# A gated cross-attention layer on one core: query blocks eight ahead of the units instead of nine, and the first output chunk split beside query blocks

## The reference, cut to what matters

```python
def _L0_xattn_ref(latents, context, Wq, Wk, Wv, Wo, q_norm_w, k_norm_w):   # (8,100,1024), (8,361,1024)
    kv = concatenate([context, latents], axis=1)                           # 461 rows a batch
    q = rms_norm((latents @ Wq) by head, q_norm_w)                         # 32 heads of 128
    k = rms_norm((kv @ Wk) by head, k_norm_w)                              # 8 key heads
    v = (kv @ Wv) by head
    probs = softmax(einsum('bhgqd,bhkd->bhgqk', qg, k) / sqrt(128))
    out = einsum('bhgqk,bhkd->bhgqd', probs, v)
    return out @ Wo                                                        # (4096, 1024)

x = x + tanh(g_xattn[0]) * _L0_xattn_ref(_layernorm(x), ctx_4096, ...)
x = x + tanh(g_ffn[0]) * _L0_ffn_ref(_layernorm(x), ...)                   # top 2 of 8 experts, rank 16
```

## Time and profile before

| | us |
|---|---|
| median of three runs | 1689.81 |
| profiled execution | 1685.8 |
| its span in the profile | 1684.0 |
| PE busy | 1650.3 (98%) |
| DVE busy | 1176.9 (70%) |
| ACT busy | 877.3 (52%) |
| POOL busy | 889.1 (53%) |

### The profile page before, as it was taken

How to read it: one execution, slowest core, us unless ns; L and a number is a source line. 1 busy time by engine, 2 the same in 40 slices (tenths; PEclk the granted TensorE clock), 3 DMA queues, 4 the chain that set the end, 5 groups by cost and what they waited for, 6 DMA issues and landing times.

```text
span 1684.0 us, 26179 instructions
## 1 busy us (share of the span) xinstructions
PE 1650.3 (98%) x9120; PEld 1470.7 (87%) x9120; DVE 1176.9 (70%) x2054; ACT 877.3 (52%) x1663; POOL 889.1 (53%) x700
## 2 busy tenths in 40 slices
PE   7999999999999999999999999999999999999997
PEld 6788888678888879999999999999999889999995
DVE  7788886677777752677677777776766777556676
ACT  5545554544544431566666666666666666443432
POOL 1344443134434420777777777777776455563131
PEclk9999999999999999999999999999999999999999
DMA  5567778736566647556666666655556566687551
GB/s 200 157 171 235 232 207 249 194 112 188 151 180 164 159 161 235 173 166 208 197 213 198 198 204 189 191 190 180 182 171 205 187 215 218 229 281 248 222 178 58
DMA packets 238503, 323.87 MB, mean 192 GB/s; under 512 B 53300, under 2 KB 193396, under 8 KB 233380
## 3 DMA queue, kind: packets, MB, share of 16 engines
q1 hardware_dynamic: 237796, 315.65, 60.3%
q10 hardware_dynamic: 576, 6.55, 1.0%
HBM read 212.18 MB, written 109.97 MB: 191 GB/s over the span
## 4 chain that ended last, share of the span: by engine, by line
PE 89%; DVE 6%; ACT 3%; issue 2%; DMA 0%; POOL 0%; DVEq 0%; SPq 0%; ACTq 0%; POOLq 0%
PE bank L991 26%; PE bank L993 25%; PE bank L992 25%; PE bank L1129 5%; PE bank L1096 2%; PE bank L1025 1%; PE bank L1335 1%; DVE wo_lo L2024 1%; DVE mx L2004 1%; DVE at_lo L2026 1%; ACT pr L1611 1%; ACT w_hi L1427 1%; PE bank L1346 0%; DMA wr<-Wkv 0%; DVE pT_lo L1998 0%
## 5 line engine op out<-in xcount | busy, mean ns | idle before, releaser
L911 POOL TENSOR_SCALAR pr<-pr,rr 100x461 f32<-100x461 f32 x256 | 371.1, 1457 | 162.1 <-DVE rr L2019 162.1
L991 PE MATMUL bank<-w_hi,a_hi 128*128 128x512 f32 (+1 forms) x856 | 341.2, 399 | 11.0 <-DVE a_lo L1794 8.5
L993 PE MATMUL bank<-w_hi,a_lo 128*128 128x512 f32 (+1 forms) x856 | 335.2, 392 | 0.0
L992 PE MATMUL bank<-w_lo,a_hi 128*128 128x512 f32 (+1 forms) x856 | 334.3, 391 | 0.0
L1611 ACT ACTIVATE pr<-bank,nm,rq 100x461 f32<-100x461 f32 x256 | 188.7, 737 | 156.7 <-DVE nm L2010 155.0
L2004 DVE TENSOR_REDUCE mx<-bank 100x1 f32<-100x461 f32 x256 | 161.4, 631 | 78.5 <-PE bank L993 75.2
L865 POOL TENSOR_TENSOR msk<-ssk,epst 128x4 f32<-128x4 f32 (+1 forms) x60 | 22.9, 382 | 348.4 <-DVE ssk L1825 348.4
L991 PEld LDWEIGHTS bank<-w_hi,a_hi 128*128 128x128 f32 (+1 forms) x856 | 157.8, 184 | 48.4 <-issue 9.6
L993 PEld LDWEIGHTS bank<-w_hi,a_lo 128*128 128x128 f32 (+1 forms) x856 | 157.6, 184 | 38.4
L991 PE MATMUL bank<-xT_hi,wq_hi 128*128 128x400 f32 x512 | 188.3, 368 | 0.7 <-issue 0.7
L992 PEld LDWEIGHTS bank<-w_lo,a_hi 128*128 128x128 f32 (+1 forms) x856 | 158.0, 185 | 34.7
(11 more groups left out here) (159 smaller groups left out, 3556.1 us busy)
## 6 DMA issues: line engine op xcount, KB each, us to landing
kT_d<-kst SPq DMA_DIRECT2D x56, 512.0 KB, 5.6
v_d<-vst SPq DMA_DIRECT2D x56, 512.0 KB
kT<-kT_d SPq DMA_DIRECT2D x64, 361.0 KB, 4.5
kvr<-ctxT SPq DMA_DIRECT2D x44, 512.0 KB, 5.9
wq_raw<-Wq SPq DMA_DIRECT2D x32, 512.0 KB, 5.8
tb<-Wo SPq DMA_DIRECT2D x16, 1024.0 KB, 8.5
wt_d<-tb SPq DMA_DIRECT2D x16, 1024.0 KB, 7.8
wo_raw<-wt_d SPq DMA_DIRECT2D x16, 1024.0 KB, 7.4
```

What stands on the lines that cost most here:

```text
L911: pool.tensor_scalar(pr[0:NQ, u % 2, i], pr[0:NQ, u % 2, i], rr[0:NQ, i:i + 1], None, ALU.mult).then_inc(p_done, 1)
L991: pe.matmul(o, lh, rh, start=start, stop=False, skip_group_check=more)
L992: pe.matmul(o, lh, rl, start=False, stop=False, skip_group_check=more)
L993: return pe.matmul(o, ll, rh, start=False, stop=stop, skip_group_check=more)
```

## The change

`AHEAD` goes from 9 to 8, so one block fewer stands ahead of unit 0, every unit u up to 55 carries block u + 8, and `bare_slot` is gone. The squares of the last block move into unit 56. The chunk parts stay where they are (`OUT0` is 55 in both). Chunk 0 is split in three steps: its weights in units 53 and 54 (two pieces each), its heads in unit 55. For that the tiles `at_hi`, `at_lo`, `wo_hi`, `wo_lo` are divided by chunk parity and laid out anew, so that chunk 0's own parts fall on memory that is free by then, and chunk 0 is loaded in units 51 and chunk 1 in 53, instead of 53 and 54. Since the blocks come one unit later, the loads and splits of query weights change between odd and even units.

```diff
-AHEAD = 9
+AHEAD = 8
 LAST_Q = UNITS - AHEAD
-OUT0 = LAST_Q
+OUT0 = LAST_Q - 1
+FIRST_W = {LAST_Q - 3: (0, 1), LAST_Q - 2: (2, 3)}
...
-        wo_hi = at("wo_hi", WR, [P, 2, R, 512], F32R)
-        wo_lo = at("wo_lo", WR + 16 * KB, [P, 2, R, 512], F32R)
+        wo_hi = [at(f"wo_hi{k}", WR + 8 * KB * k, [P, R, 512], F32R) for k in range(2)]
+        wo_lo = [at(f"wo_lo{k}", WR + 8 * KB * (3 - k), [P, R, 512], F32R) for k in range(2)]
...
-                if u in (OUT0 - 2, OUT0 - 1):
-                    load_chunk(u - OUT0 + 2)
+                if u in (LAST_Q - 5, LAST_Q - 3):
+                    load_chunk((u - LAST_Q + 5) // 2)
...
# PE, chunk_head
-                if m < G:
+                if m == 0:
+                    pe.wait_ge(wo_lo_done, R + i + 1)
+                elif m < G:
                     pe.wait_ge(wo_lo_done, 8 * m + 2 * i + 2)
                     if o == P1:
+                        pe.wait_ge(qc_done, 2 * H)
                         pe.wait_ge(ms_done, 2 * G)
# PE, last_slot (bare_slot is removed)
                 scores(u, 0)
+                if u == LAST_Q:
+                    squares(2 * H - 1)
                 turn_probs(u - 1, 0)
# ACT, new functions
+            def first_weights(i):
+                if i == 0:
+                    act.wait_ge(wo_in[0], 16)
+                    act.wait_ge(wq_lo_done, H)
+                act.activation(wo_hi[0][:, i], wo_raw[:, 0, i], ACT.Copy).then_inc(wo_hi_done, 1)
+            def first_heads(i):
+                if i == 0:
+                    act.wait_ge(at_in[0], a_loaded(0))
+                    act.wait_ge(q_done, 2 * H - 1)
+                act.activation(at_hi[0][:, :, i * NQ:(i + 1) * NQ], at_raw[0][:, :, i * NQ:(i + 1) * NQ], ACT.Copy).then_inc(wo_hi_done, 1)
# ACT, at the end of slot, behind keep_attn
+                for i in FIRST_W.get(u, ()):
+                    first_weights(i)
+                if u == LAST_Q - 1:
+                    for i in range(R):
+                        first_heads(i)
# ACT, at the start of last_slot
+                if u == LAST_Q:
+                    query_squares(2 * H - 1)
# DVE, new functions
+            def first_weights(i):
+                dve.wait_ge(wo_hi_done, i + 1)
+                dve.tensor_tensor(wo_lo[0][:, i], wo_raw[:, 0, i], wo_hi[0][:, i], ALU.subtract).then_inc(wo_lo_done, 1)
+            def first_heads(i):
+                dve.wait_ge(wo_hi_done, R + i + 1)
+                dve.tensor_tensor(at_lo[0][:, :, i * NQ:(i + 1) * NQ], at_raw[0][:, :, i * NQ:(i + 1) * NQ],
+                                  at_hi[0][:, :, i * NQ:(i + 1) * NQ], ALU.subtract).then_inc(wo_lo_done, 1)
# DVE, last_slot
                 maxima(u, 0)
+                if u == LAST_Q:
+                    copy_queries(2 * H - 1)
+                    mean_squares(2 * H - 1)
                 p_split(u - 1, 0)
# PE, ACT and DVE
-            for u in range(OUT0):
+            for u in range(LAST_Q):
                 slot(u)
-            bare_slot(OUT0)
             for u in range(OUT0 + 1, UNITS):
                 last_slot(u)
```

More of the change, by code:

```diff
@@ L259, in build @@
         wo_raw = at("wo_raw", TMP, [P, 2, R, 512])
-        at_hi = at("at_hi", HI, [P, 2, TB, QW], F32R)
-        at_lo = at("at_lo", HI + 12800, [P, 2, TB, QW], F32R)
+        at_hi = [at(f"at_hi{k}", HI + 12800 * k, [P, TB, QW], F32R) for k in range(2)]
+        at_lo = [at(f"at_lo{k}", HI + 12800 * k + 6400, [P, TB, QW], F32R) for k in range(2)]
         oT_late = at("oT_late", HI + 25600, [P, C, TW])
@@ L1212, in slot @@
                 c_(7)
[L1214 to L1227, removed]
             def last_slot(u):
@@ L1310, in last_half @@
                     mm = three(ps[n][:, 0:TW].rearrange("p (b q) -> p b q", b=TB),
-                               wo_hi[:, k, i, n * P:(n + 1) * P], wo_lo[:, k, i, n * P:(n + 1) * P],
-                               at_hi[:, k, :, i * NQ:(i + 1) * NQ], at_lo[:, k, :, i * NQ:(i + 1) * NQ],
+                               wo_hi[k][:, i, n * P:(n + 1) * P], wo_lo[k][:, i, n * P:(n + 1) * P],
+                               at_hi[k][:, :, i * NQ:(i + 1) * NQ], at_lo[k][:, :, i * NQ:(i + 1) * NQ],
                                False, i == R - 1)
@@ L1627, in chunk_piece @@
                     act.wait_ge(wo_used, R * (m - 2) + i + 1)
-                act.activation(wo_hi[:, k, i], wo_raw[:, k, i], ACT.Copy).then_inc(wo_hi_done, 1)
-                act.activation(at_hi[:, k, :, i * NQ:(i + 1) * NQ], at_raw[k][:, :, i * NQ:(i + 1) * NQ], ACT.Copy).then_inc(wo_hi_done, 1)
+                act.activation(wo_hi[k][:, i], wo_raw[:, k, i], ACT.Copy).then_inc(wo_hi_done, 1)
+                act.activation(at_hi[k][:, :, i * NQ:(i + 1) * NQ], at_raw[k][:, :, i * NQ:(i + 1) * NQ], ACT.Copy).then_inc(wo_hi_done, 1)
             def chunk_weights(m):
@@ L1635, in chunk_weights @@
                     act.wait_ge(wo_used, R * (m - 1))
-                act.activation(wo_hi[:, k], wo_raw[:, k], ACT.Copy).then_inc(wo_hi_done, 1)
+                act.activation(wo_hi[k][:], wo_raw[:, k], ACT.Copy).then_inc(wo_hi_done, 1)
             def chunk_heads(m):
@@ L1642, in chunk_heads @@
                     act.wait_ge(at_in[m % 4], a_loaded(m))
-                act.activation(at_hi[:, m % 2], a_raw(m), ACT.Copy).then_inc(wo_hi_done, 1)
+                act.activation(at_hi[m % 2][:], a_raw(m), ACT.Copy).then_inc(wo_hi_done, 1)
             def accumulators(o):
@@ L2080, in slot @@
                     next_wq(n)
-            def bare_slot(u):
-                maxima(u, 0)
-                p_split(u - 1, 0)
-                copy_queries(2 * H - 1)
-                maxima(u, 1)
-                inverse(u, 0)
-                p_split(u - 1, 1)
-                inverse(u, 1)
-                maxima(u, 2)
-                p_split(u - 1, 2)
-                inverse(u, 2)
-                maxima(u, 3)
-                p_split(u - 1, 3)
-                inverse(u, 3)
-                mean_squares(2 * H - 1)
-                q_split(u + 1)
-                for i in range(R):
-                    chunk_piece(0, i)
+                for i in FIRST_W.get(u, ()):
+                    first_weights(i)
+                if u == LAST_Q - 1:
+                    for i in range(R):
+                        first_heads(i)
             def last_slot(u):
```

14 lines of the change are left out of this document (7 added, 7 removed).

## The result

The changed kernel takes 1693.19 us (median of ten runs, 1692.11 to 1697.24) against 1689.11 us for the kernel before on the same chip (ten runs, 1687.13 to 1690.82). The ratio is 1.0028, 95% interval 1.002 to 1.0036: 4.1 us slower, where no change was forecast. The time lies just inside the stated range, at its upper end. A second series of eleven runs on another occasion gave 1692.31 against 1689.55 (31 runs), 1.0017 (1.0007 to 1.0026), 2.8 us.

The account below looks back on a forecast made before the run. The matrix engine (PE) has no idle time in the steady units. Terms -0.6 + 0 + 0.6 + 0.4 = +0.4 us give 1686.2 against the profiled execution; the median is 4.0 above that, so 1690.2, range 1685.4 to 1693.2.

Parts of the forecast that it names:

- the middle: Query units between front and back, where weight splits move from odd to even units: no cost charged, 0 us.
- the period in the middle grows: Sign of a wrong prediction: units 1 to 53 no longer 11.37 us apart.
- the front: Query blocks ahead of unit 0, and unit 0: 2.0 us gained, 1.4 lost to half clock, -0.6 us.
- the back: Units 55 and 56, with chunk 0's heads and the last squares: 27.8 us against 27.41, +0.4 us.
- the lock case: Even units: DVE's split waits for POOL's extra sum, +5 us, 1695.2 us in all; chance 0.08.
- the upper guess: Front: eight POOL sums at 1.34 us each make unit 0's rq 1.7 us earlier, a gain of 3.2.
- The third rival: Slower, DVE and POOL in even units: split waits for POOL's extra sum, 0.3 us in 16 units, +5; chance 0.08.
- Weights of chunk 0 in units 53 and 54: ACT's two added copies behind keep_attn delay DVE's maximum: 0.3 us of PE in units 54 and 55 each, +0.6.
- the last rival: Gap before squares(63) brings low clock: +1.9 instead of +0.4, +0.6 more in units 54 and 55; 1692.3; chance 0.11.
- S + 3.85: Unit 56: chunk 0's first part starts 3.85 us after S, the unit's first score on PE; 1.66 in unit 57.

Follow-up runs that it names:

- experiment 1: Changed kernel with the query-weight splits on ACT and DVE put back in odd units: 1688.64 us, ratio 1.0001 against the kernel before.
- experiment 4: Changed kernel with chunk 0's weight and head copies on ACT ahead of keep_attn in units 53 to 55: 1690.78 us, ratio 1.0017 against the kernel before.
- experiment 5: Changed kernel with POOL's six second weight sums moved to odd units, splits staying in even ones: 1691.98 us, ratio 1.0013 against the kernel before.
- experiment 7: Changed kernel with splits in odd units and chunk 0's copies ahead of keep_attn, front unaltered: 1687.03 us, ratio 0.9985 against the kernel before.
- experiment 8: Changed kernel run once more, unaltered: 1692.31 us, ratio 1.0017 against the kernel before.
- experiment 2: Kernel before with only the query-weight splits moved to even units: 1696.6 us, ratio 1.0047 against the kernel before.
- experiment 3: Changed kernel with the eight weight sums ahead of unit 0 cut to 8 of 512 columns (output wrong): 1685.79 us, ratio 0.9985 against the kernel before.
- experiment 6: Changed kernel with splits in odd units, chunk 0's copies ahead of keep_attn, only four sums ahead of unit 0's rq: 1684.02 us, ratio 0.9969 against the kernel before.

## Why the prediction was wrong

The step that failed is the middle, where I wrote "I charge nothing" for the split of the query weights in even units. DVE's split stood behind POOL's sums there and ended only 1.08 us after them, which made seven units longer by 3.0 us, of +3.3 us in all. Of the signs that the prediction named for being wrong, the last one came, "the period in the middle grows". That 1693.19 still lies inside the stated range, by 0.01 us, is luck: the range was built from the bounds of the front and the back and left the lock case out. All terms, as they stood and as they came out:

- *Front*, predicted -0.6 (bounds -3.2 and +0.1). rq still came behind the sums, PE waited 2.4 to 3.8 us (predicted about 4) and the clock fell. Counted from the landing of tb, where POOL's sums start, scores(1, 0) came at 22.96 us in both profiles with the old front, and in six with the changed one at 21.27 to 22.95, mean 22.4: -0.5. Right as a mean, but no profile shows it. The first nm came 2.2 to 2.3 us earlier, as assumed (2.0); the eight sums did get quicker, 11.58 to 11.75 us against 12.40, by less than the 1.7 of the upper guess. What half clock then took back came in two sizes. In two profiles (after, experiment 1) PE ran at half clock for some 3 us of unit 0, and 0.6 to 1.0 us were lost between nm and scores(1, 0) against the 7.40 before; in four (experiments 4, 5, 7 and 8) it ran so for some 7 us, 2.2 us were lost, and next to nothing was gained. I had charged 1.4 once. Unit 0 of experiment 8, at a mean clock of 0.77:

```profile
681.00:695.84 14.84, 11.09 (x44) 9.85 (x45) 5.89 (x16) 5.19 (x11) 10.94 (x8) 0.77 0.72 210
```

- *Middle*, predicted 0, measured +3.3 for units 1 to 53. With unit 54 it is +3.4 (617.49 to 617.60 in four profiles, 614.17 to 614.28 in four with the splits in odd units). I looked at unit 8, whose extra sum takes 1.05 us, and took DVE's free time there as cover enough. It nearly was: behind that sum alone the next unit's first maximum came 0.45 us late, just within the slack, and all but one of those units kept their length. I didn't look at the other even units. Six of them have a second weight sum of 1.49 us, which the text of the kernel names, and which in the trace before stood beside q_lo alone. There the same mechanism has no cover.
- The third rival named that mechanism, DVE's split waiting for POOL's sum, with its point of decision, "from the point at which the split ends after 785.65". It gave it 0.08, 16 units and 0.3 us each, 5 us. It came true in 7 units at 0.36 to 0.46, 3.0 us, of which 6 were not among the 16. The argument that I set against it, "the longest split of all 32 is 1.47 us", was empty: before, no split started behind one of these POOL sums, so the row couldn't show the collision. What could show it were rows that I had read as a mere lengthening: q_lo with 1.35 us where it takes 0.90. The Trainium skill ("SBUF — State Buffer", section "SBUF: two separate sides") says that a DVE instruction with two inputs from SBUF and a GpSimd instruction that reads SBUF share a port pair as an exclusive lock, and that whichever starts first holds it for the whole instruction. The traces agree for the split (1.08 us behind the sum's end twice) and for nm (0.01 us behind it). They don't agree in every row as listed: q_lo of unit 2 started 1.24 us ahead of the sum (716.23 against 717.47) and still took 1.58 us, where it takes 0.90 in units with no such sum behind it. The rule deserved more than 0.08.
- *Weights of chunk 0 in units 53 and 54*, predicted 0.3 in each of units 54 and 55. Unit 54 took 11.44 us against 11.35 before, unit 55 11.47 against 11.40 in experiment 4, where the copies are out of the way: 0.1 each. Mis-sized, within the bounds. The first maxima were 0.52 and 0.51 us late, as worked out (0.55), and the slack was some 0.44; the rest of my 0.3, "a semaphore's way", is shown by no run.
- *Back*, units 55 and 56, predicted +0.4 (27.8). Where the clock stayed up: 27.80 and 27.61. Where it fell: 28.88, 29.17 and 29.17, +1.5 to +1.8. The gap, its cause and the S + 3.85 were right, and the last rival (clock lost at the back too) is what happens in some executions. As a mean of five that is +1.1, and it holds the 0.1 of unit 55.

Together -0.5 + 3.3 + 0.1 + 1.1 = +4.0 us, against 4.1 and 2.8 measured. The middle decides: with the splits in odd units and all else unchanged, the kernel is where the forecast had it, +0.1 us against +0.4.

Unit 11, behind a sum of 1.05 us like its neighbours', is 0.36 longer. DVE has 0.30 us of idle time there ahead of pT_lo (the row at 813.07), put down to issue. Such idle time is not new. The timeline of DVE in units 11 and 33 of the kernel before:

```profile
809.13 0.16 DVE L2010 SCALAR_TENSOR_TENSOR nm<-mx,rq 100x1 f32<-100x1 f32 x1 [0.49 <-DVE mx L2004]
...
1059.45 0.57 DVE L1998 TENSOR_TENSOR pT_lo<-bank,pT_hi 121x400 fp32r<-121x400 f32 x1 [0.30 <-ACT pT_hi L1602]
```

The nm of other odd units has 0.13 there, and pT_lo next to none, yet both units kept the usual length. In experiment 2, the same kernel with the splits moved, the same two units have the same idle times (0.48 and 0.30), and both are 0.36 longer. So the idle time costs nothing while the first maximum is in time, and costs about its own length once the late split has used up the slack: unit 11 too is a loss of the split's place.

What stays open: what makes DVE idle in those few places. In experiment 2, 2 of the 8 us have no place. The medians of the changed kernel differ by 4.1 us from those before in one series and by 2.8 in the other; the clock in unit 0 and in unit 56 can differ from one execution to the next, and so can the last piece of the table, but one profile a kernel can't say which of them made the two series differ. In experiment 3, the pieces that the change touches sum to -5.7 + 3.4 + 1.8 = -0.5, and the medians say -2.8; neither was followed further.

## What to carry to other kernels

When a change moves an instruction to other turns of a loop, go through all turns that it lands in, not through one that looks typical: the turns differ in what the other engines do there, and the loss was in seven of fifty-four. A collision of DVE with POOL can't be priced from rows in which the two never stood side by side; where DVE's instruction starts second, ask when POOL's whole instruction ends. A small lateness can be free and the next one not: the 0.45 us in unit 9 cost nothing, the same 0.45 with 0.3 us of idle time on top cost 0.36 in unit 11. And where an engine has just waited about as long as a batch of copies takes (ACT's 1 us ahead of keep_attn), the batch belongs in front of that wait: with the same eight copies behind it the units 55 and 56 took 0.2 to 1.8 us more than before the change, and with them ahead of it 1.0 less.

## What the runs showed of the hardware

- A DVE subtraction over 1024 columns took 1.23 us alone, 2.10 beside a POOL sum of 1.05 us that had started 0.03 us earlier, and 2.31 beside one of 1.49 us that had started 0.26 us earlier; nm of 0.16 us took 0.81. No idle time appears on either engine: the wait is inside the duration.
- The one that starts second can be POOL's. Before the change the split came first in the odd units and kept its 1.23 us, and POOL's rq was the one that got longer (2.47 us, against 1.67 in the changed kernel, where the split is elsewhere), without any cost, since nothing was waiting for it yet. Starting first did not protect every instruction: q_lo, listed as starting 1.24 us ahead of the sum, took 1.35 us before a sum of 1.05 and 1.58 before one of 1.49, against 0.90.
- The same gap of 0.94 or 0.95 us of PE was followed by half clock (0.51 in the window shown) in three profiles and by full clock (1.00) in two. The waits of 2.4 to 3.8 us in unit 0 were followed by a stretch at 0.50 in all six profiles that have the changed front. The gap of 1.42 us ahead of unit 1 in experiment 6 was followed by full clock.
- Matmuls in a row are listed with more than their distance (the turns with 0.25 us, 0.09 us apart), so a PE wait of a quarter of a microsecond shows neither in the waits view nor in the timeline. Waits of this kind made up the 3.0 us of the seven long units.
- The first matmul of block 0, with everything before it the same program, started between 635.93 and 639.62 us in ten profiles. Spans of single profiles are therefore worth less than pieces cut at the same instruction: the spans of before and after differ by 9.0 us, their medians by 4.1.
